# A gated delta-rule layer with its feed-forward part on one core: Gram blocks stored in halves and fetched chunk by chunk, loads split in two, and a new order on every engine

## The chip, the cores and the metric

One of the cores of a Trainium2 chip runs the whole kernel. The metric is the device time of one execution in microseconds; lower is better. TensorE's clock has two levels here, 2.4 GHz (granted clock 1.00 in the rows) and 1.2 GHz (0.50).

## The reference, cut to what matters

The input is (4, 1024, 256): four sequences of 1024 tokens, four heads of 64. A first part (attention) and a second part (feed-forward) follow one another.

```python
q = short_conv(x @ Wq.T); k = short_conv(x @ Wk.T); v = short_conv(x @ Wv.T)
beta = sigmoid(x @ Wb.T)
# delta rule, per head, chunks of c tokens; q, k normalized to length 1
A = where(tri_strict, -(kb @ k.T), 0)          # kb = k * beta, the Gram matrix of a chunk
T = solve_triangular(eye - A, eye, lower=True)
u = T @ vc;  w = T @ kb
for each chunk i:                              # the scan, with state S
    attn = where(causal, q_i @ k_i.T, 0)
    u_adj = u_i - w_i @ S
    o_i = q_i @ S + attn @ u_adj
    S = S + k_i.T @ u_adj
o = mix of three long filters (FIR) of v, the scan's o, and v
y = rmsnorm(o) @ Wo.T
# then a residual, norms, and a token-shift feed-forward:
xr, xk = mixes of x and x of the token before
out = sigmoid(xr @ W_r.T) * (relu(xk @ W_k.T)**2 @ W_v.T)
```

The kernel takes chunks of 64 tokens for the scan, 16 of them (N), each for all 4 sequences and 4 heads at once (U = 8 pairs side by side, two heads on the two halves of the 128 partitions).

## The kernel before, in words

**Stages.** First comes the value stage: norm of the input, transposes, the projection to v, its short convolution, and the windows for the filters (0 to about 100 us). Then the FIR stage, bound together on TensorE and VectorE (100 to 166 us). Then the lead: projections to q and k, convolutions, squares and Gram products of the first 8 chunks (LEAD = 8). Then eight chunk steps, each of which runs the scan of one chunk, the feed-forward part of the chunk before, and the projections of the chunk eight ahead. Last come the tail steps, without projections.

**Orders written out by hand.** Each engine has functions for its steps (`gram`, `low_first`, `scan_k` on TensorE; `conv`, `at_parts`, `rest_in` on VectorE, and so on) and three lists, `lead_step(n)`, `chunk_step(n)` and `tail_step(n)`, which call them with shifted numbers: `if 0 <= n + 25 < 8: gram(n + 25, 0)` puts Gram products of chunk n + 25 into step n. An engine runs its list strictly in order. The engines meet only through semaphores, named in the functions; the numbers n of different engines are not in step with each other.

**The solve.** The Gram matrix of a chunk, 64 x 64 for each head and sequence, is inverted in levels. Its 16 x 16 diagonal blocks are solved on GpSimd (`solve_begin`, `solve_column`, 15 columns in three parts, `solve_part`), for a group of four chunks at once (GROUP = 4, four groups). The partitions are then blocks instead of tokens, so the data goes through DRAM:

1. TensorE `gram(m, g)` in two halves g; VectorE `at_parts` takes the q part; ScalarE `gram_out(m, g)` (L859) copies the k part to `G_tok`, which holds two chunks (even and odd), and may overwrite it once the store of two chunks before has landed.
2. SP `gram_store(m)` (L364) writes one chunk, 128 partitions of 2 KB, to `g_dram` with one DMA, whose destination pattern is `[[U * C, 2], [2 * U * C, C], [1, U * C]]`.
3. SP `blocks_in(g)` (L379), after the stores of all four chunks of the group and the solve of the group before, issues 16 DMAs, 4 a chunk, that fetch the diagonal blocks to `G_blk`.
4. VectorE `blocks_scaled(g)` (L1227 to L1234); GpSimd solves (from L571 to the signal at L594).
5. SP `solved_store(g)` (L383) writes `Y_blk`, 512 KB, to `y_dram`.
6. SP `solved_in(n)` fetches for one chunk 4 solved pieces (L408) and 6 pieces of the Gram matrix off the diagonal (L399, L404), all on one semaphore.
7. VectorE `solved_turn(n)` (L1240). TensorE `low_first` (L1733) and `low_second` (L1744), VectorE `low_in`, TensorE `off_first` (L1754) and `off_second` (L1765), VectorE `off_in` (L1257) fill the parts off the diagonal.
8. The scan: TensorE `scan_k` (L1777), VectorE `rest_in` (L1265), TensorE `scan_u` (L1786), `scan_o`, `scan_state`.

Other lines: L1678 projections, L1718 `gram`, L1694 `sumsq`, L335 window loads, L344 value loads, L352 input rows.

Of the kernel before, what the change touches and what calls it, by code (L numbers as in the profile page):

```python
# [36 lines left out]
P = 128  # L37
B, L, D, H = 4, 1024, 256, 4
DK = D // H
C = 64  # L40
N = L // C
# [41 lines left out]
def build(nc, x, out, wgate, consts, smalls, wq, wk, wv, wo, wr, wfk, wfv, fl, fms):  # L83
    ctx = ExitStack()
    with ctx:
# [91 lines left out]
        def take(*shape):  # L177
# [41 lines left out]
            "solved_even_in", "solved_odd_in", "turned", "low_a", "q_low", "low_b", "low_in", "off_a", "q_off", "off_b", "w_u", "ks_mm", "rest",  # L219
# [50 lines left out]
        def _(sp):  # L270
# [89 lines left out]
            def gram_store(m):  # L360

                sp.wait_ge(s["g_tok_0"], m + 1)
                sp.wait_ge(s["g_tok_1"], m + 1)
                sp.dma_start(bass.AP(g_dram.tensor, g_dram.offset + m * P * U * C, [[U * C, 2], [2 * U * C, C], [1, U * C]]), G_tok4[:, m % 2].rearrange("p u k -> p (u k)")).then_inc(  # L364
                    s["g_odd_stored" if m % 2 else "g_even_stored"], 16)

            def blocks_in(g):

                sp.wait_ge(s["g_even_stored"], 16 * (2 * g + 2))
                sp.wait_ge(s["g_odd_stored"], 16 * (2 * g + 2))  # L370
                sp.wait_ge(s["solved"], g)
                for i in range(GROUP):
                    m = GROUP * g + i
                    for half in range(2):
                        for e in range(2):
                            at_, row = 32 * i + 16 * half, HALF * half + QTR * e
                            src = bass.AP(g_dram.tensor, g_dram.offset + m * P * U * C + row * 2 * U * C + row,
                                          [[C, 2 * U], [2 * U * C, QTR], [1, QTR]])
                            sp.dma_start(G_blk[at_:at_ + 2 * U, QTR * e:QTR * e + QTR], src).then_inc(s["g_blk_in"], 16)  # L379
# [1671 lines left out]
```

## Time and profile before

| | us |
|---|---|
| median of 3 runs (676.44 to 682.8) | 682.36 |
| profiled execution | 683.21 |
| its span, first to last instruction | 681.4 |
| TensorE busy (84% of the span) | 570.5 |
| VectorE busy (70%) | 476.9 |
| GpSimd busy (44%) | 302.8 |
| ScalarE busy (42%) | 284.4 |

The mean granted clock of TensorE is 0.919. Busy shares are averages over stages with different limits; rows by stage stand below. The DMA queues move 57.05 MB.

### The profile page before, as it was taken

To read this page: it belongs to the slowest core of one execution; us is meant where nothing else is said; L and a number is where in the kernel's file an instruction comes from. 1 tells how busy PE (TensorE), PEld (TensorE's weight loads), DVE (VectorE), ACT (ScalarE), POOL (GpSimd) and SP (SyncE) were. 2 spreads that over 40 slices of the span, in tenths; PEclk is the share of its full clock that TensorE was granted. 3 is DMA by queue.
4 is the path that set the end of the run, shared out by engine and by line. 5 is a ranking of instruction groups with operands and counts; after the bars stand their busy time and mean duration, and the time that the engine had idled before them with its cause. 6 is when DMAs were issued, how large, how long until landed. Compare 5 with 4: busy or idle time off the path is not lost.

```text
span 681.4 us, 26524 instructions
## 1 busy us (share of the span) xinstructions
PE 570.5 (84%) x11052; PEld 465.2 (68%) x11052; DVE 476.9 (70%) x1198; ACT 284.4 (42%) x719; POOL 302.8 (44%) x377
## 2 busy tenths in 40 slices
PE   1788758999996867899999949999986899999964
PEld 1566636666675656777877838787875788888753
DVE  7999775655974612876967747786874788887763
ACT  1588861113653422544544524452531444344311
POOL 4411005878010700683615328651665885655432
PEclk9999989999989675998979978897986999999988
DMA  8639324993222233223232223233123133322101
GB/s 273 185 90 259 122 74 142 213 233 71 63 68 40 64 73 51 60 64 78 48 75 50 42 38 84 62 70 65 31 57 63 29 85 67 63 54 59 34 17 31
DMA packets 122471, 57.05 MB, mean 84 GB/s; under 512 B 91760, under 2 KB 114160, under 8 KB 122352
## 3 DMA queue, kind: packets, MB, share of 16 engines
q1 hardware_dynamic: 122352, 55.35, 34.6%
q8 instruction: 88, 1.44, 0.9%
q14 instruction: 31, 0.25, 0.1%
HBM read 36.36 MB, written 18.95 MB: 81 GB/s over the span
## 4 chain that ended last, share of the span: by engine, by line
PE 43%; issue 19%; DVE 18%; POOL 9%; DMA 5%; SPq 3%; ACT 2%; POOLq 0%; DVEq 0%; ACTq 0%
PE bank L1827 8%; PE bank L1678 6%; PE bank L1599 5%; DVE cva L1081 5%; PE bank L1718 3%; PE bank L1512 3%; DMA gram_scratch<-arena 2%; SPq L379 2%; PE bank L1852 2%; PE bank L1820 2%; PE bank L1786 2%; POOL seq L590 2%; POOL seq L588 2%; PE bank L1809 2%; PE bank L1777 1%
## 5 line engine op out<-in xcount | busy, mean ns | idle before, releaser
L599 POOL TENSOR_TENSOR arena<-arena,neg_half 128x2 f32<-128x2 f32 (+1 forms) x64 | 62.7, 979 | 192.9 <-DVE arena L1283 110.8
L1200 DVE SCALAR_TENSOR_TENSOR arena<-bank,small,arena 128x256 f32<-128x256 f32 x192 | 91.6, 482 | 33.2 <-ACT arena L833 28.6
L546 POOL TENSOR_TENSOR arena<-seq,powers 128x16 f32<-128x16 f32 x16 | 47.4, 2965 | 18.7 <-DVE seq L1209 18.7
L1599 PE MATMUL bank<-arena 128*64 128x192 f32 x512 | 50.1, 338 | 4.6 <-ACT arena L723 2.2
L1174 DVE TENSOR_TENSOR seq<-bank,seq 128x384 f32<-128x384 f32 x64 | 35.2, 557 | 26.1 <-PE bank L1599 18.3
L518 POOL TENSOR_TENSOR seq<-seq 128x256 f32<-128x256 f32 x32 | 23.3, 728 | 56.6 <-DVE seq L1174 56.5
L1678 PE MATMUL bank<-arena,w_k 128*128 128x268 f32 x128 | 46.3, 520 | 0.0
L1081 DVE SCALAR_TENSOR_TENSOR cva<-bank,small,cva 128x256 f32<-128x256 f32 x96 | 39.9, 476 | 8.1 <-ACT cva L711 7.9
L833 ACT ACTIVATE arena<-bank,small 128x256 f32<-128x256 f32 x64 | 29.6, 469 | 36.1 <-PE bank L1678 36.1
L1599 PEld LDWEIGHTS bank<-arena 128*64 128x64 f32 x512 | 35.0, 139 | 14.0 <-issue 7.0
L1678 PE MATMUL bank<-arena,w_q 128*128 128x268 f32 x128 | 36.4, 421 | 1.9 <-issue 1.6
L1678 PEld LDWEIGHTS bank<-arena,w_k 128*128 128x128 f32 x128 | 31.0, 255 | 9.2 <-issue 1.7
L1852 PE MATMUL bank<-seq,w_fk 128*128 128x256 f32 x128 | 33.7, 409 | 2.9 <-DVE seq L1345 2.9
L1307 DVE TENSOR_SCALAR arena<-arena 128x256 f32<-128x256 f32 x64 | 24.4, 423 | 16.5 <-POOL arena L599 16.5
L1827 PE MATMUL bank<-w_r,seq 128*128 128x256 f32 x128 | 34.7, 419 | 0.0
L1827 PE MATMUL bank<-w_fv,seq 128*128 128x256 f32 x128 | 33.5, 407 | 0.8 <-ACT arena L926 0.8
L909 ACT ACTIVATE arena<-arena 128x64 f32<-128x64 f32 x128 | 32.2, 336 | 2.6 <-issue 1.7
L1827 PE MATMUL bank<-w_o,arena 128*128 128x256 f32 x128 | 31.9, 392 | 1.6 <-ACT arena L895 0.8
L1827 PEld LDWEIGHTS bank<-w_r,seq 128*128 128x128 f32 x128 | 26.8, 214 | 4.8
L882 ACT ACTIVATE arena<-bank 128x512 f32<-128x512 f32 x16 | 9.6, 597 | 48.9 <-PE bank L1786 48.9
L1786 PE MATMUL bank<-arena 64*64 64x64 f32 x512 | 22.2, 237 | 9.1 <-issue 7.8
L1852 PEld LDWEIGHTS bank<-seq,w_fk 128*128 128x128 f32 x128 | 24.5, 201 | 7.2 <-DVE seq L1345 3.4
(169 smaller groups left out, 1436.1 us busy)
## 6 DMA issues: line engine op xcount, KB each, us to landing
arena<-fl SPq DMA_DIRECT2D x32, 192.0 KB, 6.0
arena<-fms SPq DMA_DIRECT2D x32, 192.0 KB, 6.4
arena<-xnT_scratch SPq DMA_DIRECT2D x32, 134.0 KB, 3.4
arena<-v_scratch SPq DMA_DIRECT2D x32, 128.0 KB, 3.4
gram_scratch<-arena SPq DMA_DIRECT2D x16, 256.0 KB
arena<-x SPq DMA_DIRECT2D x64, 64.0 KB, 2.6
out<-arena SPq DMA_DIRECT2D x64, 64.0 KB
xnT_scratch<-seq SPq DMA_DIRECT2D x2, 1027.0 KB, 6.5
```

The lines of the kernel that those rows point to most:

```text
L546: pool.tensor_tensor(rk, ssel[:, slot_of(n)], powers[:, :, :], ALU.pow).then_inc(s["norms"], 1)
L599: pool.tensor_tensor(dst, src, half8 if k == U else neg_half[:, 0:k], ALU.pow).then_inc(s[dst_sem], 1)
L833: act.activation(cv[:, t], proj_bank(m, t)[:, 0:B * (C + PAD)].rearrange("p (b t) -> p b t", b=B)[:, :, PAD:], ACT.Copy, scale=conv_w[:, 1 ...
L909: last = act.activation(vp[:, u, :], v_c[:, u, :], ACT.Copy, scale=rk[:, 0, u:u + 1])
L1081: nc.vector.scalar_tensor_tensor(cva[:, i, :], bank[2 + i][:, j:j + 256], conv_w[:, 2, i, j:j + 1], cva[:, i, :], ALU.mult, ALU.add).then_ ...
L1174: nc.vector.tensor_tensor(fprod[:, q % (2 * FPAIRS), :], bank[fir_bank(q)][:, 0:2 * ROW], fgate[:, q // (TILES // 2), :], ALU.mult).then_i ...
L1200: nc.vector.scalar_tensor_tensor(cv[:, t], ps[:, :, j:j + C], conv_w[:, 1 - t // 2, t % 2, j:j + 1], cv[:, t], ALU.mult, ALU.add).then_inc ...
L1599: last = mm(out_[HH[i], hh], vwin[:, P * pr + 64 * hh + d, :], toep[:, g % NB, :, :, cin, :], start=True, stop=True)
L1678: last = mm(proj_bank(m, 2 * kind + g)[:, 0:B * (C + PAD)], w["kq"[kind]][:, kh, P * g:P * g + P], xwin4[:, m % 2, kh], start=(kh == 0), s ...
L1786: last = mm(bank[4][q, C * u:C * u + C], W_u4[q, n % 2, u, :], rest[q, u, :], start=True, stop=True)
L1827: last = mm(dst[:, 256 * j:256 * j + 256], lhs[:, kh, P * j:P * j + P], wt[:, kh, :], start=(kh == 0), stop=(kh == 1))
L1852: last = mm(bank[5][:, 256 * oh:256 * oh + 256], w["fk"][:, kh, P * oh:P * oh + P], xk[:, kh, :], start=(kh == 0), stop=(kh == 1))
```

## The change

Three changes in what is issued, and new lists for all engines.

```diff
 def gram_store(m):
     sp.wait_ge(s["g_tok_0"], m + 1)
     sp.wait_ge(s["g_tok_1"], m + 1)
-    sp.dma_start(bass.AP(g_dram.tensor, g_dram.offset + m * P * U * C, [[U * C, 2], [2 * U * C, C], [1, U * C]]), G_tok4[:, m % 2]...)
+    for hh in range(2):
+        rows = bass.AP(g_dram.tensor, g_dram.offset + (m * P + hh) * U * C, [[2 * U * C, C], [1, U * C]])
+        sp.dma_start(rows, G_tok4[HH[hh], m % 2]...)
-def blocks_in(g):
-    sp.wait_ge(s["g_even_stored"], 16 * (2 * g + 2))
-    sp.wait_ge(s["g_odd_stored"], 16 * (2 * g + 2))
-    sp.wait_ge(s["solved"], g)
-    for i in range(GROUP):
-        m = GROUP * g + i
-        ... 4 DMAs
+def block_in(m):
+    g, i = divmod(m, GROUP)
+    sp.wait_ge(s["g_odd_stored" if m % 2 else "g_even_stored"], 32 * (m // 2 + 1))
+    sp.wait_ge(s["solved"], g)
+    ... the same 4 DMAs of chunk m
-def solved_in(n):            # waits y_stored, turned, off_a: 6 Gram pieces and 4 solved pieces
+def products_in(n):          # waits g_*_stored, low_a, off_a: the 6 Gram pieces, on low_even_in / low_odd_in
+def solved_in(n):            # waits y_stored, turned, off_a: the 4 solved pieces
 # TensorE low_first: waits for both semaphores; VectorE solved_turn: 64 instead of 160 a pair of chunks
```

The order of SP, the queue of the DMAs, in the lead (the numbers of a list are chunk numbers relative to its step):

```diff
 def lead_step(n):
-    rows_in(n + 3); values_in(n + 13); window_in(n + 14); toep_late(n + 3)
-    gram_store(n + 11); solved_store(solving(n + 1)); solved_in(n + 5); blocks_in(group_first(n + 3))
+    toep_late(n + 4); block_in(n + 11); gram_store(n + 12); solved_in(n + 7); window_in(n + 15)
+    rows_in(n + 6); values_in(n + 10); solved_store(solving(n + 4)); products_in(n + 11)
 def chunk_step(n):
-    solved_in(n + 4); gram_store(n + 9); blocks_in(group_first(n + 1)); window_in(n + 11)
-    solved_store(solving(n + 1)); rows_out(n); values_in(n + 4); rows_in(n + 3)
+    gram_store(n + 11); window_in(n + 14); block_in(n + 11); rows_out(n + 2); solved_store(solving(n + 3))
+    products_in(n + 7); values_in(n + 6); rows_in(n + 5); solved_in(n + 7)
```

TensorE and GpSimd in a chunk step (VectorE and ScalarE are rearranged to match):

```diff
-TensorE: scan_k(n+1) sumsq(n+8,1) low_first(n+2) scan_u(n+1) proj(n+9,0,0..1) ffn_r(n-1) gram(n+8,1) scan_o(n+1)
-  proj(n+9,1,0) x_turn(n) proj(n+9,1,1) low_second(n+2) ffn_v(n-1) scan_state(n+1) k_turn(n+2) off_first(n+2)
-  gram(n+9,0) o_turn(n+1) ffn_k(n) off_second(n+2) sumsq(n+9,0) y_rows(n+1)
+TensorE: off_first(n+1) scan_k(n+1) ffn_r(n-1) proj(n+9,0,0) off_second(n+1) gram(n+8,1) proj(n+9,0,1) scan_u(n+1)
+  proj(n+9,1,0) scan_o(n+1) x_turn(n) ffn_v(n-1) scan_state(n+1) low_first(n+2) proj(n+9,1,1) k_turn(n+2)
+  gram(n+9,0) o_turn(n+1) ffn_k(n) low_second(n+2) y_rows(n+1) sumsq(n+9,1) sumsq(n+9,0)
-GpSimd: solve_part(n-2,2) power(n-1,"st1") solve_part(n-1,0) halo power(n-1,"st2") solve_part(n-1,1)
-  power(n,"oms") norms(n+1) direct(n+1) power(n-2,"st3") output(n-2)
+GpSimd: solve_part(n-1,0) halo power(n-1,"st2") solve_part(n-1,1) power(n,"oms") power(n-2,"st3")
+  norms(n+1) output(n-2) solve_part(n-1,2) direct(n+1) power(n,"st1")
```

On VectorE `blocks_scaled` follows `low_in(n + 1)` in a chunk step (before: it followed `ffn_out`), and in the tail it moves up to stand right behind `o_summed(n)`. `solved_turn` for a chunk is called one tail step earlier. The lists of the value stage (TensorE, VectorE, ScalarE) get a new order as well, with the same calls.

## Rows read from the trace of the kernel before

**Rows 1.** Busy time by stage: start and end, length, engines (instructions), TensorE's clock, DMA share, GB/s

```profile
203.00:258.00 55.00, 38.03 (x1009) 30.02 (x1012) 23.29 (x57) 20.35 (x57) 13.24 (x32) 0.77 0.28 57
339.00:368.50 29.50, 28.09 (x633) 23.65 (x625) 22.07 (x55) 12.93 (x34) 11.07 (x10) 0.88 0.25 55
368.50:407.00 38.50, 28.38 (x747) 24.17 (x736) 22.32 (x60) 13.44 (x35) 11.14 (x10) 0.86 0.27 50
434.30:462.00 27.70, 26.65 (x642) 22.64 (x635) 21.90 (x55) 13.01 (x34) 13.21 (x17) 0.94 0.32 79
462.00:495.20 33.20, 31.98 (x716) 26.93 (x705) 24.59 (x63) 14.05 (x36) 11.81 (x11) 0.90 0.23 49
495.20:521.70 26.50, 18.34 (x416) 15.45 (x416) 14.40 (x36) 7.49 (x20) 14.32 (x17) 0.83 0.32 58
563.00:581.80 18.80, 18.28 (x458) 15.53 (x457) 15.39 (x39) 7.72 (x20) 11.34 (x11) 1.00 0.29 58
```

**Rows 2.** Timeline of SP, 195 to 283 us: start, length, line, DMA, count

```profile
203.13 0.49 SPq L364 DMA_DIRECT2D gram_scratch<-arena  x1
210.88 8.64 SPq L379 DMA_DIRECT2D seq<-gram_scratch  x16
...
238.71 0.49 SPq L364 DMA_DIRECT2D gram_scratch<-arena  x1
239.25 0.47 SPq L383 DMA_DIRECT2D solved_scratch<-seq  x1
248.26 0.32 SPq L399 DMA_DIRECT2D arena<-gram_scratch  x1
```

**Rows 3.** Timelines of VectorE and ScalarE; in brackets idle time before and its releaser

```profile
221.00 0.18 DVE L1227 TENSOR_SCALAR seq<-seq 128x32 f32<-128x32 f32 x1 [7.57 <-DMA seq<-gram_scratch]
222.94 0.38 ACT L859 ACTIVATE arena<-bank 128x256 f32<-128x256 f32 x1 [8.02 <-issue]
```

**Rows 4.** The chain that ended last, 215 to 285 us: GpSimd's first and last piece

```profile
222.59 0.99 POOL seq L571
...
238.28 0.02 POOLq L594
```

**Rows 5.** Timeline of TensorE, 195 to 283 us

```profile
223.47 1.97 PE L1718 MATMUL bank<-seq 64*64 64x128 f32 x16 [7.02 <-ACT arena L859]
...
257.62 1.05 PE L1733 MATMUL bank<-arena,seq 16*32 16x16 f32 x64 [3.28 <-DMA arena<-solved_scratch]
...
263.71 1.97 PE L1777 MATMUL bank<-arena 64*64 64x64 f32 x32
```

**Rows 6.** DMA, 202 to 212 us (share in 40 slices), 235 to 262, 310 to 317, whole span

```profile
DMA  9992000021101120201111311111111110000003
...
solved_scratch<-seq SPq DMA_DIRECT2D x1, 512.0 KB, 9.0
...
solved_scratch<-seq SPq DMA_DIRECT2D x1, 512.0 KB, 3.1
...
arena<-v_scratch SPq DMA_DIRECT2D x32, 128.0 KB, 3.4
```

**Rows 7.** Timelines of SP, VectorE and TensorE around the blocks of group 2

```profile
380.64 0.55 SPq L364 DMA_DIRECT2D gram_scratch<-arena  x1
388.43 9.30 SPq L379 DMA_DIRECT2D seq<-gram_scratch  x16
...
400.20 0.19 DVE L1227 TENSOR_SCALAR seq<-seq 128x32 f32<-128x32 f32 x1 [10.32 <-DMA seq<-gram_scratch]
...
405.45 1.05 PE L1733 MATMUL bank<-arena,seq 16*32 16x16 f32 x64 [8.07 <-DVE arena L1257]
```

**Rows 8.** Timeline of VectorE around the blocks of group 3

```profile
516.32 0.18 DVE L1227 TENSOR_SCALAR seq<-seq 128x32 f32<-128x32 f32 x1 [7.16 <-DMA seq<-gram_scratch]
```

**Rows 9.** Timeline of TensorE, inside `scan_u` of an ordinary chunk step

```profile
369.69 0.92 PE L1786 MATMUL bank<-arena 64*64 64x64 f32 x24
372.17 0.45 PE L1786 MATMUL bank<-arena 64*64 64x64 f32 x8 [1.56 <-issue]
```

More of the change, by code:

```diff
@@ L1041, in _ @@
+                if 8 <= n < N:
+                    oT_out(n)
+                if 9 <= n + 1 < N:
+                    ktok_out(n + 1)
+                if 8 <= n < N:
+                    state_out(n)
+                if 7 <= n - 1 < N:
+                    k_square(n - 1)
+                if 9 <= n + 1 < N:
+                    off_out(n + 1)
+            for n in range(-149, 21):
                 lead_step(n)
@@ L1443, in chunk_step @@
                     x_stats(n)
+                if 0 <= n + 1 < 8:
+                    rest_in(n + 1)
+                if 1 <= n + 1 < 9:
+                    off_in(n + 1)
                 if 8 <= n + 9 < N:
                     conv(n + 9, 0)
+                    conv(n + 9, 1)
+                if 0 <= n < 8:
+                    x_normed(n)
+                if 8 <= n + 9 < N:
+                    conv(n + 9, 2)
+                if 0 <= n + 1 < 8:
+                    o_scaled(n + 1)
+                    o_summed(n + 1)
+                if 8 <= n + 8 < N:
+                    at_parts(n + 8, 1)
             def tail_step(n):
@@ L1454, in tail_step @@
                     o_summed(n)
+                if n >= 8 and solving(n) is not None:
+                    blocks_scaled(solving(n))
                 if 7 <= n - 1 < N:
@@ L1467, in tail_step @@
                     ffn_out(n - 2)
[L1468 to L1470 removed]
                     f_stats(n - 2)
+                if 9 <= n + 2 < N:
+                    solved_turn(n + 2)
                 if 9 <= n + 1 < N:
@@ L1483, in tail_step @@
                     residual(n)
-            for n in range(-133, 21):
+            for n in range(-149, 21):
                 lead_step(n)
@@ L1869, in lead_step @@
             def lead_step(n):
+                if 0 <= n + 19 < 1:
+                    low_first(n + 19)
+                if 0 <= n + 28 < 8:
+                    proj(n + 28, 0, 1)
+                if FIRST <= n + 129 <= FIRST + 8:
+                    fir_turns(n + 129, 0)
+                if n + 19 == -1:
+                    banks_cleared(n + 19)
                 if 0 <= n + 18 < 1:
-                    k_turn(n + 18)
+                    off_first(n + 18)
                 if 0 <= n + 25 < 8:
-                    gram(n + 25, 0)
+                    sumsq(n + 25, 0)
@@ L1906, in chunk_step @@
             def chunk_step(n):
+                if 1 <= n + 1 < 9:
+                    off_first(n + 1)
                 if 0 <= n + 1 < 8:
                     scan_k(n + 1)
+                if 0 <= n - 1 < 7:
+                    ffn_r(n - 1)
+                if 8 <= n + 9 < N:
+                    proj(n + 9, 0, 0)
+                if 1 <= n + 1 < 9:
+                    off_second(n + 1)
                 if 8 <= n + 8 < N:
-                    sumsq(n + 8, 1)
-                if 1 <= n + 2 < 9:
-                    low_first(n + 2)
+                    gram(n + 8, 1)
@@ L1961, in tail_step @@
                 if 9 <= n + 2 < N:
-                    k_turn(n + 2)
+                    low_first(n + 2)
                 if 8 <= n + 1 < N:
@@ L1984, in tail_step @@
                     scan_k(n + 2)
-            for n in range(-133, 21):
+                if 9 <= n + 2 < N:
+                    off_second(n + 2)
+            for n in range(-149, 21):
                 lead_step(n)
```

627 lines of the change are left out of this document (301 added, 326 removed).

## The prediction

> **What bounds the kernel now.** I read the busy times by stage first, then the queue of SyncE (SP), which issues every DMA, then the waits. Chunk step means the time between two subtractions for `rest` on VectorE (L1265). In an ordinary chunk step with projections TensorE is busy 26.65 of 27.70 us, and in an ordinary tail step, which has no projections left, 18.28 of 18.80 us [rows 1]. These stages are bound by TensorE, and a better order can win little there. Three places look different. In the stage before the first scan (203 to 258 us) TensorE is busy 38.0 of 55 us, at a mean granted clock of 0.77. The step from 368.5 lasts 38.5 us with the same TensorE work as its neighbours, and the two steps from 462 last 33.2 and 26.5 us [rows 1]. All three hang on one chain: the Gram blocks of four chunks go to DRAM, their diagonal blocks come back, VectorE scales them, GpSimd solves them. The kernel before waits for the fourth chunk's store and only then issues the sixteen block loads of all four.
>
> **The chain before the first scan, as it is.** The store of chunk 3 is issued at 203.13; the loads that wait for it begin at 210.88, so it took 7.7 us, and their issue takes 8.64 us [rows 2]. VectorE, in order, stands 7.57 us until the last has landed at 221.0 [rows 3]. Scaling takes 1.6 us, GpSimd starts at 222.59 and is done at 238.28, 15.7 us [rows 4]. The solved store is issued at 239.25, 0.54 us behind another Gram store, and the loads that wait for it begin at 248.26 [rows 2]. TensorE takes up the product that needs them at 257.62, after standing idle, and reaches the first scan product at 263.71 [rows 5]. The sixteen loads also hold back SP: the next Gram store goes out only after them, ScalarE cannot overwrite its Gram buffer and waits 8.02 us [rows 3], and TensorE stands 7.02 us [rows 5].
>
> **The store in halves.** The DMA share of the stretch from 202 to 212 us shows tenths of 1 while the store runs alone: about 2 of 16 engines [rows 6]. The old destination pattern has an outermost dimension of 2, the new ones of 64. Loads of values, 128 KB each, have a median of 3.4 us to landing, and the solved store (512 KB) takes 3.1 us when nothing slow is ahead of it but 9.0 us right behind a Gram store [rows 6]. That 9.0 is nearly the old store's own duration on top of the rest, so the narrow pattern costs twice before the first scan. For the new pair I take 1.0 us for two issues (0.49 each [rows 2]) and 2.4 us until landing. I choose this between 2.0 us (the last block load, from issue at about 219.0 to VectorE's start [rows 2, 3]) and 3.4 us (128 KB of values [rows 6]), nearer to the first because the solved store shows that long pieces go fast; the far bound is 7.8 us for the pair, no gain at all.
> The Trainium skill (DMA: Bandwidth & Descriptors, how many engines a DMA uses) says that a DMA is split over the largest number up to 16 that divides the slowest dimension of both patterns: 2 before, 16 after. The trace agrees with the 2. The same page puts a fixed 2.0 us on every DMA, which speaks against cutting one into two; but the two overlap, so here it would cost only the second issue.
>
> **Blocks chunk by chunk.** Twelve of the sixteen loads now go out after earlier stores. Behind the fourth store only four are left: 4 x 0.54 = 2.2 us (8.64 us for 16 [rows 2]) plus 2.0 us to land. Store to landing becomes 1.0 + 2.4 + 2.2 + 2.0 = 7.6 us, against 17.9 us in the first group. The price is that SP now waits for a store in every chunk. Queued behind that wait are the values, input rows and the loads for products; they are asked for a chunk or more ahead, so I count nothing. If this cover fails the price is about 3 us per step, the store's latency.
>
> **Loads for products split from solved blocks.** Six of ten loads no longer need the solved store. Behind it only four remain, 4 x 0.5 + 2.0 = 4.0 us, against 9.4 us from 248.26 to 257.62 [rows 2, 5]. In the new SP order `solved_store(0)` stands ahead of `gram_store(5)`, so chunk 5's store waits for the solve, and behind it ScalarE's `gram_out(7, 0)` and TensorE's `gram(7, 1)`, which stands before `low_first(0)`. That new wait ends at about 235: solve 228, store of the solution and four block loads 2.7 us, Gram halves 1.0 + 2.4, copy and products 1.5.
>
> **Sum for the lead.** 203.1 + 7.6 = 210.7; scaling 1.6 gives 212.3; solve 15.7 gives 228.0; store 0.5 + 3.1 gives 231.6; loads 4.0 gives 235.6. TensorE's own remaining work ends near that too: its 38.0 busy us of this stage at a mean clock of 0.77 [rows 1] are some 30 us at full clock (an estimate, 38.0 x 0.8), so 233. I take 237 for `low_first(0)` instead of 257.6, so **-20 us**. The following off-diagonal products keep their 6 us [rows 5]. The bound downward is -10 (the store as slow as before, which also delays the solved store), upward -23.
>
> **Group 2.** Issue of the store at 380.64, loads from 388.43 for 9.30 us, VectorE waiting 10.32 us until 400.20, and TensorE taking up `low_first` only at 405.45 after 8.07 us idle [rows 7]. VectorE came to its wait 9.3 us after the store was issued. In the new order `blocks_scaled(2)` comes after `low_in`, again some 9 to 10 us behind the last Gram copy (walking the step: `low_first`, a projection, `k_turn`, `gram`, `o_turn`, `ffn_k`, `low_second` on TensorE). The new 7.6 us fit below that, so the wait goes. The step is 38.5 us, against 27.7 and 29.5 for ordinary ones [rows 1]: **-10 us**. With a store of 7.8 us the wait would still be 3 to 4 us and the gain 6. What is late next is TensorE itself, with 26 to 27 us of work.
>
> **Group 3.** Here VectorE waits 7.16 us until 516.32 [rows 8]; the two steps take 59.7 us, and 27.7 + 19 to 22 would be ordinary [rows 1], an excess of about 11. In the new order `blocks_scaled(3)` is placed earlier, right after `o_summed(8)`, about 7 us behind `gram(15, 1)`. That leaves 1 to 3 us of waiting: **-8 us** (-4 to -11).
>
> **The new order elsewhere.** In the old step TensorE runs 184 small product pairs in one piece (`scan_k`, `sumsq`, `low_first`, 24 of `scan_u`) and then stands 1.56 us with nothing to wait for, [rows 9], and the mean clock of such steps is 0.88 to 0.94 [rows 1]. The new step has a piece just as dense (two `sumsq`, `off_first`, `scan_k`: 192), followed by long products. Some of the stall may be covered: I take -3 us over the eight steps, bounds -20 (all gone) and +20. `rest_in` and `off_in` must end before `scan_u`; in the new order `ffn_r`, two projection halves, `off_second` and `gram` lie between `scan_k` and `scan_u`, where only `sumsq` and `low_first` lay before, so this pair gets more cover, not less; but `off_second` now waits for a copy in the same step. On GpSimd the third part of the solve lies before `direct` and the next power: a third of 15.7 is 5 us, and GpSimd is busy only 11.07 of 29.5 us in a step without a solve [rows 1], so it fits. The order of the first 100 us changes too, with the same operations on each engine; only waits at its two ends can move, and I count zero. The FIR stage and the tail keep their operations; at 18.28 of 18.80 the tail has no more than 0.5 us a step to give [rows 1].
>
> **Total.** 683.21 (profiled execution: span 681.4 plus 1.8 around it) - 20 - 10 - 8 - 3 = 642.2. That execution lies 0.9 above the median of the runs shown, so the forecast for the median is **641 us**. A difference below 1% is about what a measurement of this kernel can't tell from none (the three runs themselves span 0.9%).
>
> **Rivals.**
> A. The halves land no faster than the whole did (7.8 us a pair). Each chain is 5.4 us longer, the first loses some 5 more on the solved store: 641 + 16 = 657. Against it speaks the share of 2 engines of 16 [rows 6]; for it that no store of just this pattern is in the trace. 0.12.
> B. The new order in the lead ties its own knot: the Gram store of chunk 5 sits behind the solved store, and TensorE falls to half clock while it waits. The lead gives 10 instead of 20: 651. The row for it is the old one of the same kind, 7.02 us of TensorE behind a Gram buffer [rows 5]. 0.15.
> C. The stalls without a releaser go as well, with their half clock (1.6 + about 1.5 us in most steps): 626. 0.15.
> D. Slower: the chain `off_first`, copy, `off_second`, `off_in`, now squeezed between `scan_k` and `scan_u` in each chunk step, ends after TensorE's cover. Then TensorE waits in each of the eight steps; from about 1 us of delay it becomes the rule, and with 3 us of idle and 3.4 us of lost clock it would be 8 x 6.4 = 51 us, so 692. Against it: VectorE is busy only 21.90 of 27.70 us [rows 1], and the two wins of the old stall steps would still have to be eaten. 0.07.
> E. The DMAs of each chunk (28 against 27) and the waits of SP starve input rows or values, 1 us a step: 641 + 15 = 656. 0.03.
> Forecast as told, with its own range 634 to 648: 0.48.
>
> **From these the numbers.** The range takes in A, B, C and the bounds of the terms, 624 to 664. Faster by over 1% is everything but D: 0.91; within 1% 0.03 (D half as large); slower 0.06.
>
> **What the profile will show.** Right: Gram stores in pairs, four block loads 3 us after each; DMA share well above 1 tenth in them; `low_first(0)` before 240; the wait of VectorE for Gram blocks, 25.05 us in total before (7.57 + 10.32 + 7.16 [rows 3, 7, 8]), below 6; the step of group 2 under 30 us. Wrong: block loads 7 us or more behind their store; ScalarE or TensorE standing at the copy of chunk 7; or a wait in front of `scan_u` in ordinary steps.

## The result and the profile after

| | before | after |
|---|---|---|
| median | 682.58 us (676.44 to 683.3, 4 runs) | 649.32 us (647.69 to 652.12, 4 runs) |
| profiled execution | 683.21 us | 647.69 us |
| its span | 681.4 us | 645.9 us |
| mean granted clock | 0.919 | 0.950 |

The ratio to the kernel before is 0.954, with a 95% interval of 0.949 to 0.958: faster by 33 us. The forecast was 641, the range 624 to 664. Medians here and below leave out two disturbed executions, one of x4_both (892.5 us, granted clock 0.56) and one of x5_all_old_lists (662.7 us); with them those medians are 659.5 and 654.0.

To see where the time went, I lay the starts of the same TensorE work of both kernels side by side: `low_first(0)`, and `y_rows(n)`, the output projection of chunk n, once in each step. The column of differences is what the new kernel gained in that stretch (minus) or lost (plus). One trace of each kernel stands behind it, and the start of `low_first(0)` moves by 3 us and more between executions with the same lead lists: it is 236.9, 237.0, 236.5 and 240.2 in the four kernels below that leave the lead of the change as it is.

| stretch | before | after | difference | predicted |
|---|---|---|---|---|
| start to `low_first(0)` | 257.62 | 236.87 | -20.7 | -20 |
| `low_first(0)` to `y_rows(0)` | 24.9 | 26.3 | +1.3 | 0 |
| four ordinary steps, `y_rows` 0 to 4 | 111.1 | 112.9 | +1.8 | small, -3 over all |
| step of group 2, `y_rows` 4 to 5 | 37.4 | 26.9 | -10.4 | -10 |
| `y_rows` 5 to 7 | 57.2 | 54.5 | -2.7 | part of the -3 |
| two steps of group 3, `y_rows` 7 to 9 | 52.2 | 48.3 | -3.9 | -8 |
| from `y_rows(9)` to the end | 141.0 | 140.1 | -0.9 | 0 |

**The lead.** This is the stretch before the first scan. First SP's timeline in the kernel after, lines of the queue that [rows 2] shows for before:

```profile
204.47 1.12 SPq L366 DMA_DIRECT2D gram_scratch<-arena  x2
205.76 1.08 SPq L335 DMA_DIRECT2D arena<-xnT_scratch  x2
207.38 1.79 SPq L379 DMA_DIRECT2D seq<-gram_scratch  x4
...
227.96 0.34 SPq L383 DMA_DIRECT2D solved_scratch<-seq  x1
228.39 2.26 SPq L379 DMA_DIRECT2D seq<-gram_scratch  x4
230.75 1.82 SPq L366 DMA_DIRECT2D gram_scratch<-arena  x2
232.68 2.18 SPq L420 DMA_DIRECT2D arena<-solved_scratch  x4
```

The two halves of chunk 3's store go out at 204.47, and the four block loads that wait for them at 207.38, 2.9 us later; before, sixteen loads followed 7.75 us behind the store [rows 2]. VectorE and TensorE of the same kernel, against [rows 3] and [rows 5]:

```profile
210.64 0.19 DVE L1251 TENSOR_SCALAR seq<-seq 128x32 f32<-128x32 f32 x1 [4.15 <-DMA seq<-gram_scratch]
...
234.97 1.97 PE L1737 MATMUL bank<-arena 64*64 64x128 f32 x16 [3.27 <-ACT arena L880]
236.87 1.05 PE L1753 MATMUL bank<-arena,seq 16*32 16x16 f32 x64
```

VectorE takes up the blocks at 210.64 (the sum said 210.7), SP sends the solution off at 227.96 (228.0), and `low_first(0)` starts at 236.87 (237). The wait in front of it is the predicted new one, `gram(7, 1)` behind chunk 5's store, and it ends at 234.97 (about 235). The DMA view of the kernel after, 203 to 214 us in 40 slices of 0.28 us, shows the halves themselves; before, the store alone showed 1 tenth [rows 6]:

```profile
DMA  4330032414989868999546252520000000000000
...
gram_scratch<-arena SPq DMA_DIRECT2D x4, 128.0 KB, 2.3
```

For about 1.1 us from 205.75 the 16 engines are mostly 8 to 9 tenths busy, and a half has landed 2.3 us after its issue (2.4 predicted).

**The steps.** Busy times by stage of the kernel after, columns as in [rows 1]: the lead, an ordinary step, the step of group 2, the one behind it, the two steps of group 3 (which straddle the change from chunk steps to tail steps), and a tail step.

```profile
203.00:237.00 34.00, 28.17 (x653) 21.51 (x653) 20.09 (x49) 17.48 (x53) 17.26 (x35) 0.90 0.35 72
...
320.00:348.90 28.90, 27.36 (x629) 22.53 (x629) 22.97 (x55) 12.75 (x35) 11.35 (x11) 0.94 0.29 59
...
376.00:402.90 26.90, 25.77 (x628) 21.34 (x629) 24.28 (x59) 12.71 (x35) 21.80 (x34) 1.00 0.29 61
...
402.90:430.40 27.50, 25.83 (x629) 21.40 (x629) 22.37 (x55) 12.77 (x35) 14.63 (x20) 1.00 0.34 74
...
457.40:484.50 27.10, 22.47 (x596) 18.78 (x596) 17.98 (x47) 10.00 (x31) 14.81 (x14) 0.94 0.32 62
484.50:505.80 21.30, 18.25 (x453) 15.56 (x453) 15.57 (x38) 7.76 (x21) 18.48 (x30) 1.00 0.20 39
543.40:562.20 18.80, 18.15 (x452) 15.53 (x452) 15.56 (x40) 7.70 (x21) 11.34 (x10) 1.00 0.28 58
```

The step of group 2 is now as short as any, 26.9 us with the solve in it. The tail step has not changed, 18.8 us as in [rows 1]. The ordinary step shown, from 320 us, still takes 28.9 us at a clock of 0.94; the one behind it takes 27.1 us at 1.00. The two steps of group 3 keep some 4.6 and 3 us in which TensorE has no work. The waits view of the kernel after (who waits for whom: total, times, longest):

```profile
DVE seq L1251 <- DMA seq<-gram_scratch: 4.6, 2, 4.1
...
PE bank L1797 <- issue: 7.7, 7, 1.4
```

VectorE's waits for Gram blocks fell from 25.05 us to 4.6. The stalls of TensorE that nothing releases are there as before; in the chunk steps only their place moved, from `scan_u` (six with 7.8 us in total, one of them in [rows 9]) to `scan_k` (L1797, seven with 7.7 us) and once `off_first` (1.12 us at 463.45).

### The profile page after: what moved, and what is told of

Same layout as the page of the kernel before. It is cut to its first block, busy times and chain, and to the rows that moved or that the text cites. A ratio compares the mean times of both kernels' runs of the same rounds, so it can differ in the third digit from the quotient of the medians.

```text
span 645.9 us, 26569 instructions
## 1 busy us (share of the span) xinstructions
PE 558.2 (86%) x11052; PEld 450.6 (70%) x11052; DVE 483.4 (75%) x1198; ACT 282.3 (44%) x719; POOL 302.6 (47%) x377
## 4 chain that ended last, share of the span: by engine, by line
PE 33%; DVE 22%; issue 19%; POOL 15%; SPq 4%; DMA 4%; ACT 2%; POOLq 0%; DVEq 0%; ACTq 0%
PE bank L1847 7%; PE bank L1618 6%; DVE cva L1106 5%; POOL arena L616 4%; PE bank L1697 3%; POOL arena L563 3%; POOL seq L607 3%; POOL seq L605 3%; PE bank L1840 3%; PE bank L1872 2%; DVE arena L1224 2%; DVE arena L1312 2%; DVE arena L1319 2%; DVE seq L1094 2%; PE bank L1532 2%
## 5 line engine op out<-in xcount | busy, mean ns | idle before, releaser
L616 POOL TENSOR_TENSOR arena<-arena,neg_half 128x2 f32<-128x2 f32 (+1 forms) x64 | 62.5, 977 | 177.1 <-DVE arena L1307 102.5
L1198 DVE TENSOR_TENSOR seq<-bank,seq 128x384 f32<-128x384 f32 x64 | 35.2, 557 | 28.9 <-PE bank L1618 17.3
L563 POOL TENSOR_TENSOR arena<-seq,powers 128x16 f32<-128x16 f32 x16 | 47.5, 2970 | 0.0
L854 ACT ACTIVATE arena<-bank,small 128x256 f32<-128x256 f32 x64 | 29.9, 469 | 37.0 <-PE bank L1697 37.0
L1697 PE MATMUL bank<-arena,w_k 128*128 128x268 f32 x128 | 38.9, 442 | 3.3 <-DMA arena<-xnT_scratch 3.2
L1369 DVE SCALAR_TENSOR_TENSOR seq<-seq,small,arena 128x256 f32<-128x256 f32 x64 | 38.0, 646 | 0.3
L576 POOL TENSOR_TENSOR arena<-arena,gates 128x512 f32<-128x512 f32 x16 | 17.8, 1114 | 35.0 <-issue 33.9
L1697 PEld LDWEIGHTS bank<-arena,w_k 128*128 128x128 f32 x128 | 25.5, 210 | 10.7 <-DMA arena<-xnT_scratch 4.0
L1847 PE MATMUL bank<-w_fv,seq 128*128 128x256 f32 x128 | 31.5, 390 | 0.8 <-ACT arena L947 0.8
L922 ACT ACTIVATE arena<-bank 128x256 f32<-128x256 f32 x32 | 10.5, 381 | 47.6 <-PE bank L1862 43.7
```

Of the source, the lines that this page charges most:

```text
L563: pool.tensor_tensor(rk, ssel[:, slot_of(n)], powers[:, :, :], ALU.pow).then_inc(s["norms"], 1)
L616: pool.tensor_tensor(dst, src, half8 if k == U else neg_half[:, 0:k], ALU.pow).then_inc(s[dst_sem], 1)
L854: act.activation(cv[:, t], proj_bank(m, t)[:, 0:B * (C + PAD)].rearrange("p (b t) -> p b t", b=B)[:, :, PAD:], ACT.Copy, scale=conv_w[:, 1 ...
L1198: nc.vector.tensor_tensor(fprod[:, q % (2 * FPAIRS), :], bank[fir_bank(q)][:, 0:2 * ROW], fgate[:, q // (TILES // 2), :], ALU.mult).then_i ...
L1369: nc.vector.scalar_tensor_tensor(dst[:, hf].rearrange("p (b t) -> p b t", b=B), dx[:, hf].rearrange("p (b t) -> p b t", b=B), mu[:, i, hf: ...
L1697: last = mm(proj_bank(m, 2 * kind + g)[:, 0:B * (C + PAD)], w["kq"[kind]][:, kh, P * g:P * g + P], xwin4[:, m % 2, kh], start=(kh == 0), s ...
```

## The experiments

Two theories stood against each other at the start. **The DMA theory**, that of the prediction: the gain comes from the three DMA edits, each worth its term, and the new order brings little. **The order theory**: the DMA edits alone free time that the old lists cannot take up, since VectorE and SP reach the freed work no earlier. The recorded expectations call them chain theory and lists theory. A third question was what the ordinary steps lose. Each kernel below ran beside the kernel before on the same chip, whose median stands in the table too; gains in the text are differences to that median. Differences between kernels of different chips are given by both ways of counting. The table also lists, from the traces, the start of `low_first(0)` and three stretches between `y_rows`.

| kernel | median us | before, same chip | ratio, 95% | `low_first(0)` | 1 to 4 | 4 to 5 | 7 to 9 |
|---|---|---|---|---|---|---|---|
| before | 682.6 |  |  | 257.6 | 86.0 | 37.4 | 52.2 |
| after | 649.3 | 682.6 | 0.949 to 0.958 | 236.9 | 85.9 | 26.9 | 48.3 |
| x1_halves | 668.0 | 680.8 | 0.978 to 0.989 | 249.5 | 83.7 | 31.6 | 50.2 |
| x3_early | 672.4 | 680.8 | 0.982 to 0.992 | 256.9 | 85.9 | 31.0 | 49.4 |
| x4_both | 657.4 | 680.8 | 0.963 to 0.973 | 250.2 | 82.6 | 27.8 | 48.5 |
| x5_all_old_lists | 651.0 | 680.8 | 0.953 to 0.966 | 247.6 | 86.6 | 27.9 | 47.5 |
| x2_whole | 671.1 | 679.1 | 0.980 to 0.994 | 255.2 | 80.6 | 30.3 | 52.6 |
| x6_store_first | 648.3 | 679.1 | 0.948 to 0.957 | 237.7 | 85.0 | 27.8 | 49.0 |
| x7_broken_run | 635.6 | 679.1 | 0.929 to 0.945 | 237.0 | 77.2 | 26.5 | 47.2 |
| x8_seam | 653.6 | 679.1 | 0.955 to 0.966 | 240.2 | 83.0 | 27.0 | 55.7 |
| y1_best | 639.6 | 682.6 | 0.932 to 0.944 | 241.4 | 77.2 | 26.5 | 47.9 |
| y2_both_ahead | 644.1 | 682.6 | 0.941 to 0.952 | 236.5 | 79.0 | 26.5 | 48.9 |
| y3_before_broken | 673.2 | 682.6 | 0.983 to 0.993 | 255.2 | 76.3 | 40.6 | 52.4 |
| y4_old_lists_broken | 650.6 | 682.6 | 0.950 to 0.960 | 246.6 | 76.3 | 31.0 | 47.5 |

The trace of x5_all_old_lists is that of the execution of 662.7 us, so its stretches are only a rough guide.

### 1. The halves alone (x1_halves)

The kernel before, with its store and counts changed:

```diff
-sp.dma_start(... [[U * C, 2], [2 * U * C, C], [1, U * C]] ...)      # in gram_store, one DMA
+for hh in range(2): sp.dma_start(... [[2 * U * C, C], [1, U * C]] ...)
 # waits for the stores: 32 a chunk instead of 16
```

> The kernel before with the Gram store in two halves and nothing else. Chain theory (the time between a group's last Gram store and its solve is what is won): each store lands 4.3 us sooner (7.7 to 3.4), the solved store some 6 us sooner (9.0 to 3.1): low_first(0) 10 us earlier, groups 2 and 3 by 4.3 each: 682.6 - 19 = 664. Rival (the gain lies in the new lists, the DMA work is hidden): 680 to 683. Rival (the halves land no faster): 682.

Measured 667.95 us, 13 faster (19 forecast). In the lead VectorE's wait for the blocks is 4.33 us instead of 7.57 [rows 3], and `low_first(0)` comes 8.1 us earlier. The timeline of SP in this kernel shows what the halves don't reach:

```profile
203.97 1.09 SPq L366 DMA_DIRECT2D gram_scratch<-arena  x2
207.31 9.80 SPq L381 DMA_DIRECT2D seq<-gram_scratch  x16
...
236.38 0.58 SPq L385 DMA_DIRECT2D solved_scratch<-seq  x1
```

The loads start 3.3 us behind the store, but sixteen of them still take 9.8 us of SP.

### 2. The early loads alone (x3_early), and both (x4_both)

`blocks_in` of the kernel before is cut into `block_in(m)`; in groups 0, 2 and 3 the first three chunks' loads go out right before the next Gram store, the fourth's where `blocks_in` stood. x3_early has the whole store, x4_both the halves as well. The lists of the other engines are the old ones.

```diff
 def lead_step(n):
+    if 0 <= n + 10 < 8: early_block(n + 10)      # not group 1, not the last chunk of a group
     if 0 <= n + 11 < 8: gram_store(n + 11)
```

> The kernel before with an undivided store; the block loads of the first three chunks of groups 0, 2 and 3 go out before the next Gram store, only four are left behind the last. Chain theory: 12 x 0.54 = 6.5 us less in each of three chains, though SP waits for every store now: 682.6 - 18 = 665. If the waits of SP for the slow stores cost more than that: 675 or above. Lists theory: 680 to 683.

> Both of these, in the old lists. Chain theory: lead -16, group 2 -10 (the wait of VectorE for blocks gone), group 3 -6: 651, close to the changed kernel (649.3). Lists theory: 665 or more. The wait of VectorE for Gram blocks should fall from 25 us to below 6.

Early loads alone gave 8 us (18 forecast), both together 23 us (32 forecast). In x3_early the lead gained only 0.7 us: VectorE takes up the blocks at 223.56 after 7.88 us of waiting, later than before [rows 3]. The slow store now lies in every chunk's path: the block loads of each chunk wait for it in SP's queue, ahead of the next store. Its gain is in group 2, 6.4 us. In x4_both the DMA part of the sum holds: the last four loads are issued at 209.62 and take SP 2.0 us. But then, SP first and VectorE second:

```profile
209.62 2.01 SPq L379 DMA_DIRECT2D seq<-gram_scratch  x4
...
235.10 0.58 SPq L391 DMA_DIRECT2D solved_scratch<-seq  x1
240.09 0.33 SPq L407 DMA_DIRECT2D arena<-gram_scratch  x1
...
246.96 0.43 SPq L416 DMA_DIRECT2D arena<-solved_scratch  x1
```

```profile
213.65 2.94 DVE L1212 SCALAR_TENSOR_TENSOR arena<-bank,small,arena 128x256 f32<-128x256 f32 x6
216.51 0.18 DVE L1239 TENSOR_SCALAR seq<-seq 128x32 f32<-128x32 f32 x1
```

VectorE starts on the blocks at 216.51 with no wait before it. They had been there since about 213.6 (the last load, plus 2.0 us to land). VectorE had convolutions to do first, since the old list has them ahead of `blocks_scaled`. The solution is stored at 235.10 instead of 227.96, and ten loads behind it take from 240.09 to 247.4. `low_first(0)` comes at 250.2, 13 us later than in the kernel after. Of the 7.1 us between the two solutions, about 3 are blocks that landed later (213.6 against 210.6) and 2.9 are VectorE, busy until 216.51. The DMA theory's -20 for the lead does not come from store and loads alone, and in this the order theory is right. But it is wrong that the DMA edits bring little.

### 3. All three DMA edits on the old lists (x5_all_old_lists)

x4_both with the product loads cut from the solved ones, as in the change, `products_in(n)` ahead of `solved_store` in the lead and ahead of `solved_in` in the steps.

> All three DMA edits of the change (halves, early blocks, loads for products split from solved blocks) in the old lists. Chain theory: 3 us less than the run without the split, since six of ten issues leave the path behind the solved store before the first scan only: 648, the same as the changed kernel within 1%. If the new lists carry a part of the gain: 655 or more.

Measured 651.0 (648 forecast), 6.4 below x4_both (3 forecast). `low_first(0)` moved up by 2.6 us only, to 247.6. Six of ten loads are gone from behind the solution, whose store is issued at 236.01; the last of the four solved loads ends its issue at 243.56 and has landed some 2 us later. TensorE then comes to `low_first(0)` without a wait for them: ahead of it in the old list stands a piece of 256 `sumsq` pairs, in which it stands twice for 1.58 us. The ratio to the kernel before is 0.959 against 0.954 for the change, 4 us apart, and their intervals overlap. So by the totals the three DMA edits bring at least 23 us of the 33, and whether the new lists add to them is not settled by this pair; experiment 7 settles it.

### 4. The change without the halves (x2_whole)

```diff
-for hh in range(2): sp.dma_start(... [[2 * U * C, C], [1, U * C]] ...)
+sp.dma_start(... [[U * C, 2], [2 * U * C, C], [1, U * C]] ...)
```

> The changed kernel with the undivided Gram store. Chain theory: each store lands 4 us later and the solved store waits behind the store of chunk 4 or not at all; low_first(0) 5 to 9 us later, groups 2 and 3 by 2 to 4 each: 649.3 + 14 = 663. If the halves were of no use in the new order: 650.

Measured 671.08: the whole store costs 22 to 25 us in the new kernel, by the medians and by the gains on each chip (forecast 14). `low_first(0)` comes at 255.2, 18 us later. TensorE's timeline shows waits that no step of the sum had:

```profile
209.96 3.23 PE L1695 MATMUL bank<-arena,w_k 128*128 128x268 f32 x8 [2.38 <-DMA arena<-xnT_scratch]
...
222.32 3.94 PE L1695 MATMUL bank<-arena,w_k 128*128 128x268 f32 x8 [3.28 <-DMA arena<-xnT_scratch]
...
235.84 2.07 PE L1695 MATMUL bank<-arena,w_k 128*128 128x268 f32 x8 [1.85 <-DMA arena<-xnT_scratch]
...
253.25 1.97 PE L1735 MATMUL bank<-arena 64*64 64x128 f32 x16 [4.08 <-ACT arena L878]
```

The first three are waits for the windows of the projections, which are issued behind a block load that waits for its store; the fourth is one for the Gram buffer of [rows 5]. With a store of 7.7 us the per-chunk wait starves TensorE; with halves of 2.3 us it costs nothing that the trace shows. Cutting the loads by chunk is worth much only with a short store: with the whole store, x3_early gained 8 us, and so did this kernel, with the new lists besides; x4_both gained 23.

### 5. The new wait ahead of `low_first(0)` (x6_store_first)

In the new lead list the Gram store of chunk 5 goes ahead of the solved store, and the block loads of chunks 4 to 7 behind it.

```diff
-    block_in(n + 11); gram_store(n + 12); solved_in(n + 7); window_in(n + 15); ... solved_store(solving(n + 4))
+    if n + 11 < 4: block_in(n + 11)
+    gram_store(n + 12); solved_store(solving(n + 3)); solved_in(n + 7)
+    if n + 11 >= 4: block_in(n + 11)
```

> The changed kernel with the Gram stores of chunks 5 to 7 and the solved loads moved ahead of the block loads of group 1 on SP, and the store of chunk 5 ahead of the solved store. In the changed kernel TensorE stands 3.3 us before gram(7, 1) for it and the solved loads are issued 4.7 us after the solved store. Theory: low_first(0) 2 to 3 us earlier and as much on the time, 647. Rival: the time is lost again in the first two steps, which are bound by GpSimd's solve of group 1: 649, same.

Measured 648.34 (647 forecast), not to be told from the change; `low_first(0)` at 237.7. The wait of 3.27 us is gone. That `low_first(0)` is no earlier does not show that the wait cost nothing, since in this execution VectorE takes up the blocks at 213.43 instead of 210.64, as late as in x8_seam (214.22), whose lead is that of the change. Counted from there, `low_first(0)` comes after 24.2 us instead of 26.2, 2.0 us sooner, as forecast. Whether that reaches the total is open: the medians differ by 1 us.

### 6. The dense run of small products (x7_broken_run, y2_both_ahead, y3_before_broken)

In the ordinary steps of the kernel after, TensorE's timeline reads:

```profile
290.06 1.97 PE L1847 MATMUL bank<-w_o,arena 128*128 128x256 f32 x8
291.95 1.29 PE L1713 MATMUL bank<-cst,arena 64*32 64x4 f32 x128
293.17 0.69 PE L1774 MATMUL bank<-arena 32*32 32x32 f32 x32
293.79 0.92 PE L1797 MATMUL bank<-arena 64*64 64x64 f32 x24
295.75 0.69 PE L1797 MATMUL bank<-arena 64*64 64x64 f32 x8 [1.04 <-issue]
296.37 3.78 PE L1847 MATMUL bank<-w_r,seq 128*128 128x256 f32 x8
```

128 pairs of `sumsq`, 32 of `off_first`, 24 of `scan_k`: after 184 pairs TensorE stands, as after 184 in the kernel before [rows 9]. In the other chunk steps the count is 166 to 187 here and 165 to 185 before. (A pair is the weight load and the matmul of one small product.) The eight long products behind it take 3.78 us, and 1.97 the eight ahead of it: the clock has fallen to its lower level, 1.2 GHz. The mean granted clock from 293.2 to 300 us is 0.65. But the clock does not fall behind every such stall. Two steps on, the same eight products take 1.99 us:

```profile
354.71 0.45 PE L1797 MATMUL bank<-arena,seq 64*64 64x64 f32 x7 [0.98 <-issue]
355.09 1.99 PE L1847 MATMUL bank<-w_r,seq 128*128 128x256 f32 x8
```

It is so behind the last five of these stalls. In x2_whole, which has TensorE's lists of the change and its stalls (0.76 to 1.20 us), the mean granted clock from 281.6 to 472.2 us is 1.00. What brings it down in the first steps stays open.

What the stall waits for can be guessed from the DMA view of the kernel after, 293.3 to 294.5 us:

```profile
q8 instruction: 1, 0.02, 5.0%
```

Besides the queue of the data the profile shows one that carries instructions. Here it moved one packet of 16 KB, which ended at 294.41, and TensorE went on at 295.75, 1.34 us later. Each of the eight stalls in the chunk steps of this kernel ends 1.2 to 1.5 us after the end of such a packet, and so does each of the six in the kernel before, while such a packet comes only every 5 to 6 us on average. This speaks for TensorE waiting for its own instructions there; no run shows it by a change.

x7_broken_run moves one half of `sumsq` ahead of `y_rows`:

```diff
+    sumsq(n + 9, 0)
     y_rows(n + 1)
     sumsq(n + 9, 1)
-    sumsq(n + 9, 0)
```

> The changed kernel with one of the two sumsq of a chunk step moved ahead of y_rows, so that the longest run of small products falls from 192 pairs to 128. If the stall without a releaser (about 1.1 us in each chunk step) comes from the density of the run, it goes or shrinks below 0.5 us: 649.3 - 8 = 641. If it comes from the average number of instructions and not the longest run, nothing moves: 649.

Measured **635.55 us** (641 forecast), 14 below the change by the medians and 10 by the gains on each chip; x6_store_first, on the same chip, is 13 above it. TensorE's timeline and the busy times by stage in this kernel:

```profile
289.89 1.99 PE L1847 MATMUL bank<-w_o,arena 128*128 128x256 f32 x8
291.82 0.71 PE L1713 MATMUL bank<-cst,arena 64*32 64x4 f32 x64
292.46 0.69 PE L1774 MATMUL bank<-arena 32*32 32x32 f32 x32
293.08 1.15 PE L1797 MATMUL bank<-arena 64*64 64x64 f32 x32
294.16 1.99 PE L1847 MATMUL bank<-w_r,seq 128*128 128x256 f32 x8
```

```profile
289.90:315.80 25.90, 25.64 (x634) 21.27 (x629) 21.36 (x52) 12.84 (x35) 13.78 (x17) 1.00 0.37 79
315.80:341.50 25.70, 25.57 (x636) 21.27 (x629) 23.09 (x55) 12.77 (x35) 11.36 (x11) 1.00 0.34 67
```

In a full step the longest run is now 128 pairs. From `y_rows(0)` on no stall without a releaser is left in the chunk steps (one of 0.65 us stands just before it, in the first step, which has no `ffn_k`), their clock is 1.00, and a step takes 25.7 to 27.0 us instead of 26.9 to 29.9. Set beside the change's step from 320 us, 28.9 us long: TensorE's idle time goes from 1.5 to 0.1 us, and its busy time for the same work from 27.36 to 25.57. The second part, 1.8 us, is the clock, which is 0.94 there and 1.00 here. From `y_rows(0)` to `y_rows(3)`, where the change's clock is 0.87 to 0.94, the gain is 10.2 us; over the four steps behind, where both have 1.00, it is 3.7 us.

> Control for broken_run: the changed kernel with both sumsq of a step ahead of y_rows, so that the run of 192 small pairs stands before y_rows (low_second, two sumsq) and only 64 behind it (off_first, scan_k). Density theory: a stall of about 1 us in each step is back, now at the end of the first run or right behind, and the time is 645 to 650. Rival (broken_run won because one sumsq, or what waits for it, came earlier): no stall, 636 or less.

y2_both_ahead puts both halves of `sumsq` ahead of `y_rows`, behind the 64 pairs of `low_second`: 192 pairs in one run. It measured 644.1, in between: 4.5 above y1_best on the same chip. Eight stalls are back, 3.8 us in total, but not where and not as long as the density theory (that the stall comes from the length of the run) had them. After one of 1.37 us in the first step, seven of 0.35 us stand behind only 64 pairs, ahead of the two `sumsq`:

```profile
288.79 1.27 PE L1713 MATMUL bank<-cst,arena 64*32 64x4 f32 x128 [0.35 <-issue]
```

The clock of these steps is 1.00. So a run of 192 pairs alone does not make the stall of 1 us; what stands around it counts too, and the rule by length is not shown.

> The kernel before with low_first moved behind scan_u and two projection halves in the chunk steps; the run of 184 small pairs, in which TensorE stands 1.05 to 1.56 us, becomes 128. Density theory: the stalls go, and the half clock behind them: six steps x (1.3 idle + about 1.7 of clock) = 18, of which the steps with a VectorE wait give back little: 682 - 13 = 669. Rival (the old order has its stalls from something else, or waits for low_first grow instead): 680 or more.

y3_before_broken is the kernel before with `low_first` behind the next projection, so that the longest run there is 128 pairs (`scan_k`, `sumsq`, `scan_u`). The three ordinary steps go from 86.0 to 76.3 us, without a stall and at a clock of 1.00. One stall of 1.03 us is left in the first step, behind `low_first` with its 64 pairs, and no such packet of instructions ends near it. In total it gained only 9 us (673.2; 669 forecast), since part came back as a wait: its VectorE stands 12.99 us for the blocks of group 2 (10.32 before [rows 7]), and TensorE behind it:

```profile
403.33 1.97 PE L1786 MATMUL bank<-arena 64*64 64x64 f32 x32 [13.86 <-DVE arena L1265]
```

A faster TensorE reaches the same slow chain earlier. That step grew from 37.4 to 40.6 us.

### 7. What the new lists are worth (y4_old_lists_broken)

x5_all_old_lists with the same cut of the dense run as y3_before_broken, to compare old and new lists where hardly a stall blurs the steps.

> The old lists with all three DMA edits (654.0) and the same move of low_first. Density theory: 654 - 13 = 641. The rest up to broken_run on the new lists (635.5) would be what the new lists are worth without the stalls: some 6 us, mostly in front of the first scan, where VectorE comes to the blocks earlier and the solved loads are not behind others.

Measured 650.55 (641 forecast). That is no clear gain over x5_all_old_lists (651.0; by the ratios 0.955 against 0.959, and the intervals overlap), so on these lists the cut of the run brought far less than forecast. Against x7_broken_run (635.55), which has the same DMA edits and no stalls in these steps either, the old lists cost 15 us by the medians and 11 to 13 by the gains and ratios on each chip (some 6 to 19 by the two intervals): 9.6 in the lead (`low_first(0)` at 246.6 against 237.0) and 4.5 in the step of group 2 (31.0 against 26.5). The second is a chain wait as in y3_before_broken: VectorE stands 3.33 us for the blocks and TensorE 4.26 us for VectorE. In the lead it is not VectorE and SP alone. The last solved load ends its issue at 242.12 us and has landed some 2 us later, but TensorE is still in its 256 `sumsq` pairs and comes to `low_first(0)` without a wait:

```profile
246.32 0.28 PE L1722 MATMUL bank<-cst,arena 64*32 64x4 f32 x7 [1.86 <-issue]
246.56 1.05 PE L1762 MATMUL bank<-arena,seq 16*32 16x16 f32 x64
```

So some 2.4 us of the 9.6 are TensorE's own list, with its stalls. The ordinary steps are the same, 76.3 against 77.2.

### 8. The place between chunk steps and tail steps (x8_seam, y1_best)

The two steps of group 3 won 3.9 us of the 8 predicted. VectorE's timeline of the kernel after shows that the wait for the blocks is not the reason:

```profile
475.15 0.19 DVE L1251 TENSOR_SCALAR seq<-seq 128x32 f32<-128x32 f32 x1 [0.41 <-DMA seq<-gram_scratch]
...
484.70 0.71 DVE L1264 STREAM_TRANSPOSE arena<-arena 128x512 f32<-128x512 f32 x1 [3.90 <-DMA arena<-solved_scratch]
...
496.51 0.77 DVE L1331 TENSOR_SCALAR arena<-arena 128x256 f32<-128x256 f32 x2 [3.50 <-POOL arena L616]
```

It was 7.16 us [rows 8] and is 0.41. What is late next: solved pieces for which SP came late (its queue is full from 468 to 483 us with a Gram store, block loads, output rows, values and products ahead of them), and a `power` of GpSimd that stands behind a third of the solve. x8_seam moved that third behind the power, in the tail steps:

```diff
-    solve_part(n - 1, 1)          # at the end of GpSimd's tail step
+    solve_part(n - 2, 1)          # one step on, behind power(n - 2, "st2") and halo
```

> The changed kernel with the second third of group 3's solve on GpSimd moved behind the power and the copy that x_turn(8) waits for. In the changed kernel VectorE waits 3.5 us for that power and TensorE 2.5 us. Theory: 2 to 3 us less, 647. Rival: something else is as late there (the values of chunk 9, the solved pieces of chunk 10): 649, same.

Measured 653.63 (647 forecast), not better. The wait on L616 went, but the one for solved pieces grew to 6.15 us and others appeared further on; the two steps took 55.7 us. So the power is not the cause by itself. That the solved pieces come too late from SP is what the trace suggests; no run tried it.

> The two edits of store_first and broken_run together, on the changed kernel. Theory: the times are won at different places (the lead, the chunk steps) and add: 635.5 - 1 = 634, the fastest of all. Since the first was worth 1 us at most, it may be the same as broken_run alone: 636.

y1_best has the edits of x6_store_first and x7_broken_run: 639.6 us (634 forecast), not to be told from x7_broken_run alone (635.6, intervals overlap). The fastest by its median is x7_broken_run, the change with one `sumsq` moved: 44 us below before on its chip, where the change gained 33 on another.

## Why the prediction was right, and where not

- **The lead, -20.** Right, -20.7, in part by luck. VectorE's start (210.7, row 210.64), the solution (228.0, 227.96) and `low_first(0)` (237, 236.87) fit, but the store went out at 204.47 and not at 203.1, and from it to VectorE's start it took 6.2 us and not 7.6: two errors that cancel. The loads behind the solution go out at 232.68, 1.1 us later than in the sum. The same lead lists gave 240.2 in another execution. And the attribution was wrong. The text put it down to the DMA edits. With these on the old lists `low_first(0)` moves up by 7 to 11 us (x4_both, x5_all_old_lists, y4_old_lists_broken). The other 10 came only with the new lists. The sum had assumed this silently, in "210.7; scaling 1.6 gives 212.3": VectorE had to be free at 210.7. In the old list it isn't until 216.5 (x4_both), which is about 3 us behind the blocks; the rest is SP's order and TensorE's 256 `sumsq` ahead of `low_first(0)`. No run moves VectorE's call alone.
- **The halves.** 2.4 us predicted, 2.3 measured. Rival A priced their failure at 16 us; x2_whole shows 22 to 25. The missing part goes with the wait in SP's queue, where "I count nothing" held for short stores only.
- **Group 2, -10.** Right, -10.4. VectorE takes up the blocks without a wait. Here the DMA edits do nearly all: x4_both and x5_all_old_lists, on the old lists, have 27.8 and 27.9 us for this step against 26.9. Only with a faster TensorE does the list count for more (31.0 against 26.5 in y4_old_lists_broken).
- **Group 3, -8.** This term was mis-sized: -3.9. The wait on the blocks fell to 0.41 us, even more than "1 to 3 us of waiting". But the sum took most of the excess of the two steps as due to it. The solved pieces behind a full SP queue and a power behind the solve took its place; which of them sets the end stays open (experiment 8).
- **The new order elsewhere, -3.** The ordinary steps gave -0.9 (+1.8 and -2.7), inside the bounds. The reasoning "some of the stall may be covered" was wrong: the stalls in the steps are as long as before, with a run just as dense in the new list. Another +1.3 came between `low_first(0)` and `y_rows(0)`, which the sum had at 0.
- **The total.** The profiled execution was forecast at 642.2 and took 647.7, 5.5 more: 4.1 of group 3, 2.1 of the order, 1.3 behind `low_first(0)`, less 2.0 that the lead, group 2 and the end gave beyond their terms. The median lies another 1.6 above that execution, where the forecast had put it 1 below.
- **The rivals.** B came true as a wait and hardly as a price: the Gram buffer's 3.27 us stand ahead of `low_first(0)`, and taking them away brings it at most 2 us forward (x6_store_first). C put 15 us on the stalls and their clock, and x7_broken_run gained 10 to 14 with them gone. But the change doesn't remove them, and that the clock hangs on them is not shown. D did not come: in ordinary steps no wait for `rest` stands in front of `scan_u`. E did not show with halves; with the whole store it is a part of what x2_whole lost.

## What to carry to other kernels

When a chain of DMA round trips is shortened, check for each link that the engine that takes it up is free at that moment in its own list; half of the gain in the lead came only with the new lists and not with the DMAs. A wait for a store in a queue that issues everything is cheap only as long as the store is short, so shorten the store first and split the waits after. Before reordering, look for stalls that nothing releases: see whether a packet of the instruction queue ends just before they do, and try a long product in the middle of the dense run ahead of them. That one line was worth 10 to 14 us in the new kernel and 9 in the kernel before, about as much as the halves alone (13), but hardly anything on the old lists with the DMA edits, so it has to be measured each time.

## What the runs showed of the hardware

- **Runs of small products.** In the chunk steps of the kernels before and after, TensorE stood 0.93 to 1.56 us, waiting for nothing that the profile names, after 165 to 187 products of at most 64 x 64 weights in one piece, in two quite different orders. With such a piece cut to 128 these stalls went (x7_broken_run, y3_before_broken). Length is not all of it: a piece of 192 in y2_both_ahead had only 0.35 us, behind its first 64, and one stall of 1.03 us in y3_before_broken stood behind 64.
- **Instructions come by DMA.** All 14 of those long stalls ended 1.2 to 1.5 us after a 16 KB packet of the profile's instruction queue had ended, with 88 packets on that queue in the whole execution. That TensorE waited for instructions is inferred from these times.
- **The clock behind a stall.** After 1.04 us of it eight products took 3.78 us, at 1.2 GHz, instead of 1.99 at 2.4 GHz; after 0.98 us two steps later they took 1.99. In the same order in x2_whole the clock stayed at 1.00 through all such stalls. So the stall alone does not bring it down.
- **A DMA whose outermost dimension is 2.** 128 partitions of 2 KB took 7.7 us on about 2 of 16 engines [rows 2, 6]. As two DMAs with 64 outermost they took 2.3 us each, overlapped, with 8 to 9 tenths of the 16 engines busy. It also delays what comes behind it: the solved store took 9.0 us after it and 3.1 without [rows 6]. By the rule of the Trainium skill (DMA: Bandwidth & Descriptors, "How many engines (k)") the first runs on 2 engines and the others on 16, and both traces agree; the delay of the DMA behind it is this case's own number.
